# The opening of an attention stage re-dealt: four routed rows requested at once, late tiles, fills, loads and one batch's normalization put in other slots

## The reference, cut to what matters

```
x = x + tanh(g_xattn[0]) * quantized_linears(layernorm(x))
x = x + tanh(g_ffn[0])   * moe0(layernorm(x))       # 8 experts, top 2, and a shared expert for every row
x = x + tanh(g_xattn[1]) * attention(layernorm(x))  # q = x @ Wq, rope, 32 heads of 16, 512 keys, softmax, @ Wout + bout
x = x + tanh(g_ffn[1])   * moe1(layernorm(x))       # 8 experts, top 2
```

## Time and profile before

| | us |
|---|---|
| median of 3 runs | 1315.97 (1313.9 to 1318.4) |
| the profiled execution | 1319.94 |
| its span from first to last instruction | 1318.2 |
| attention block starts at | 561.8 |
| first reduction of the maxima | 623.06 |
| first scores, turn (0, 0) | 669.2 |

### The profile page before, as it was taken

How to read it: one execution, slowest core, us unless ns; L and a number is a source line. 1 busy time by engine, 2 the same in 40 slices (tenths; PEclk the granted TensorE clock), 3 DMA queues, 4 the chain that set the end, 5 groups by cost and what they waited for, 6 DMA issues and landing times.

```text
span 1318.2 us, 16527 instructions
## 1 busy us (share of the span) xinstructions
PE 1159.4 (88%) x5247; PEld 509.5 (39%) x5309; DVE 831.5 (63%) x1289; ACT 666.5 (51%) x1175; POOL 397.7 (30%) x469
## 2 busy tenths in 40 slices
PE   5777776899999999958799989999999999889997
PEld 3454443555444444423232223222322222224543
DVE  6798765235555554136978888777877777714543
ACT  2565554565222222236456666666656666763452
POOL 4466531002322222043234432222222223102332
PEclk8988898999999999988899999999999999999999
DMA  7424125644544444194324342222222225400101
GB/s 239 134 99 136 56 89 183 234 178 163 208 135 142 155 149 132 62 292 101 107 80 138 114 122 79 83 81 80 75 86 79 80 81 65 51 5 9 38 35 48
DMA packets 111029, 145.79 MB, mean 111 GB/s; under 512 B 24952, under 2 KB 79736, under 8 KB 110440
## 3 DMA queue, kind: packets, MB, share of 16 engines
q1 hardware_dynamic: 91816, 113.47, 26.7%
q0 software_dynamic: 18368, 28.85, 8.5%
q10 hardware_dynamic: 768, 2.49, 0.6%
HBM read 99.54 MB, written 48.37 MB: 112 GB/s over the span
## 4 chain that ended last, share of the span: by engine, by line
PE 32%; DVE 9%; issue 8%; ACT 7%; POOL 1%; DMA 1%; ACTq 0%; POOLq 0%; DVEq 0%
PE PS L2888 7%; PE PS L2854 5%; PE PS L2789 4%; PE PS L2873 4%; PE PS L2813 3%; DVE a_top L3223 3%; ACT shared_w L3010 2%; PE PS L2391 2%; PE PS L2414 1%; ACT a_E L3010 1%; DMA a_attnT<-f_y,l_pos 1%; POOL a_K L2151 1%; PE PS L2018 1%; DVE a_early L3096 1%; PE PS L1984 1%
## 5 line engine op out<-in xcount | busy, mean ns | idle before, releaser
L3223 DVE TENSOR_REDUCE a_top<-PS 128x2 f32<-128x1024 f32 x256 | 309.2, 1223 | 84.9 <-PE PS L2873 78.5
L3010 ACT ACTIVATE shared_w<-PS 128x512 f32<-128x512 f32 x256 | 138.9, 596 | 74.7 <-PE PS L2854 73.8
L2854 PE MATMUL PS<-a_Q,a_K 99*128 99x512 bf16 (+1 forms) x468 | 156.9, 387 | 15.7 <-ACT a_E L3010 3.4
L3010 ACT ACTIVATE a_E<-PS 128x512 f32<-128x512 f32 x256 | 138.8, 596 | 61.1 <-PE PS L2854 57.9
L1502 PE MATMUL PS<-f_W,f_GT 128*128 x312 | 141.3, 596 | 0.0
L2873 PE MATMUL PS<-a_K,a_Q 64*128 64x512 bf16 x512 | 100.8, 390 | 13.4 <-DVE a_top L3223 7.0
L1931 POOL TENSOR_TENSOR a_qf<-a_qf,a_tab 128x512 f32<-128x512 f32 x15 | 19.1, 1272 | 279.9 <-DVE a_swapped L3125 279.9
L2854 PEld LDWEIGHTS PS<-a_Q,a_K 99*128 99x128 bf16 (+1 forms) x512 | 44.1, 97 | 151.2 <-issue 49.6
L1558 DVE TENSOR_TENSOR f_H<-f_SG,PS 128x256 f32<-128x256 f32 x39 | 16.4, 421 | 115.3 <-ACT f_SG L1542 115.3
L1502 PEld LDWEIGHTS PS<-f_W,f_GT 128*128 128x128 f32 x312 | 56.7, 191 | 57.2 <-issue 57.2
L2789 PE MATMUL PS<-a_xT,a_early 128*128 128x512 f32 x128 | 72.4, 662 | 2.2 <-ACT a_qf L2982 0.8
(11 more groups left out here) (381 smaller groups left out, 2085.7 us busy)
## 6 DMA issues: line engine op xcount, KB each, us to landing
f0r_raw<-in_L_ffn_W_dram SPq DMA_DIRECT2D x24, 512.0 KB, 4.0
a_K<-k_parts SPq DMA_DIRECT2D x192, 64.0 KB, 2.3
a_Q<-a_q_parts SPq DMA_DIRECT2D x186, 64.0 KB
f_y<-f_Y SPq DMA_DIRECT2D x39, 256.0 KB, 2.0
v_units<-V SPq DMA_DIRECT2D x16, 512.0 KB, 2.9
a_V<-v_units SPq DMA_DIRECT2D x16, 512.0 KB, 3.5
k_parts<-f_k_parts SPq DMA_DIRECT2D x16, 384.0 KB, 3.4
a_q_parts<-a_parts SPq DMA_DIRECT2D x16, 384.0 KB, 2.8
```

Source lines behind the costliest of these rows:

```text
L2854: nc.tensor.matmul(PS[:, 4 + h % 2, :], K6[k][0:rows_, o, head // 2, kt * P:(kt + 1) * P], Q6[k][0:rows_, o, head // 2, :], start=True, st ...
L3010: nc.scalar.activation(E[step % 2][:, h, :], PS[:, 4 + h % 2, :], ACT.Exp).then_inc(exp_done, 1)
L3223: nc.vector.tensor_reduce(top[:, h - h % 2:h - h % 2 + 2, t], PS[:, 2 * pair:2 * pair + 2, :], AX.X, ALU.max).then_inc(maxed, 1)
```

## The change

The ring of routed rows gets a fourth slot, so that the gathers of tiles 0 to 3 are all requested at once; tiles 8 to 15 are added one turn later each. Batch 0 is measured and normalized before the loop, each `bn_stats` behind its tile. The late tiles' loads come in four pieces with a semaphore each. SyncE waits for tile 0 before it requests Wq, and for tile 2 before the bias (now first), the table, K, V and the late tiles' second load. The transposes of batch 0 alternate between banks 7 and 3. Late tile 2 stops after two of its ups before the loop; the tables `LATE` and `FILLS` are dealt anew, and ScalarE's six loads of q come at slot 4 behind the silus, instead of slot 3. Batch 1 is measured at slots 8 to 13 of turn (-1, 3), normalized at slots 4 to 7 of turn (0, 0), transposed at slots 8, 10, 12 and 14 there, its bias added in four pieces at slots 12 to 15.

```diff
 class LateTiles
-    DOWN = (6, 0, 1, 2, 6, 6, 6, 6)
+    DOWN = (6, 0, 1, 6, 6, 6, 6, 6)
     def load(self, sp, k):
-        sp.dma_start(self.homes[k], self.xT_dram[k]).then_inc(self.loaded[k], 16)
+        for c in range(self.DC):
+            sp.dma_start(self.homes[k][:, c, :], self.xT_dram[k][:, c, :]).then_inc(self.loaded[k][c], 16)
     def up(self, pe, n, c):
+        if t == 0:
+            pe.wait_ge(self.loaded[k][c], 16)
 attention
-        rows = Combine(..., 3, [attnT[1][:, d, :] for d in range(DC)])
+        rows = Combine(..., 4, [attnT[1][:, d, :] for d in range(DC)])
 jobs
-                for d, when in enumerate((6, 7, 8, 10)):
+                for d, when in enumerate((8, 10, 12, 14) if b == 0 else (6, 7, 8, 10)):
                     add(when, "x", (b + 1, 0), d)
-        LATE = {(-1, 0): {9: [("g", 2, 0), ("y", 0, 0), ("y", 1, 0), ("t", 2, 0)]},
-                (-1, 2): {4: downs(2) + ups(3), 5: [("g", 3, 0), ("y", 2, 0)] + ups(4), 6: [("t", 3, 0), ("g", 4, 0)] + downs(3),
-                          7: [("y", 3, 0), ("t", 4, 0)], 8: downs(4, [0]), 9: downs(4, [1]), 10: [("y", 4, 0)] + ups(5, [0]), 11: ups(5, [1]),
-                          12: ups(5, [2]), 13: ups(5, [3]), 14: [("g", 5, 0)], 15: [("t", 5, 0)]},
-                (-1, 3): {4: downs(5), 5: [("y", 5, 0)] + ups(6, [0]), 6: ups(6, [1]), 7: ups(6, [2]), 8: ups(6, [3]), 9: [("g", 6, 0)],
-                          10: [("t", 6, 0)] + ups(7, [0]), 11: ups(7, [1]), 12: ups(7, [2]) + downs(6, [0]), 13: ups(7, [3]),
-                          14: downs(6, [1]) + [("g", 7, 0)], 15: [("y", 6, 0), ("t", 7, 0)]},
+        LATE = {(-1, 0): {9: [("y", 0, 0), ("y", 1, 0)]},
+                (-1, 2): {4: ups(2, [2, 3]) + ups(3), 5: [("g", 2, 0), ("t", 2, 0)] + downs(2), 7: [("y", 2, 0), ("g", 3, 0)],
+                          8: [("t", 3, 0)] + ups(4, [0]), 9: downs(3), 10: ups(4, [1]), 11: [("y", 3, 0)] + ups(4, [2]),
+                          12: ups(4, [3]), 13: [("g", 4, 0)] + ups(5, [0]), 14: [("t", 4, 0)] + ups(5, [1]), 15: ups(5, [2])},
+                (-1, 3): {4: ups(5, [3]) + downs(4, [0]), 5: downs(4, [1]) + ups(6, [0]), 6: [("g", 5, 0), ("y", 4, 0)] + ups(6, [1]),
+                          7: [("t", 5, 0)] + ups(6, [2]), 8: ups(6, [3]) + downs(5, [0]), 9: downs(5, [1]),
+                          10: [("g", 6, 0), ("y", 5, 0)] + ups(7, [0]), 11: [("t", 6, 0)] + ups(7, [1]), 12: ups(7, [2]) + downs(6, [0]),
+                          13: ups(7, [3]) + downs(6, [1]), 14: [("g", 7, 0), ("y", 6, 0)], 15: [("t", 7, 0)]},
                 (0, 0): {0: downs(7), 1: [("y", 7, 0)]}}
 bank_of
+            if kind == "x" and unit[0] == 0:
+                return PS[:, (7, 3)[extra % 2], :]
 batch_to_norm
-            nb = {0: b + 1 if b == -1 else None, DC - 1: b + 2}.get(c)
+            nb = {0: b + 1 if b < 1 else None, DC - 1: b + 2 if b >= 0 else None}.get(c)
 sync
             late.load(sp, 0)
+            sp.wait_ge(rows.tile_added, 1)
             sp.dma_start(wq, ...)
+                    else:
+                        sp.wait_ge(rows.tile_added, TB - 1)
+                        sp.dma_start(tbias[:], bout.partition_broadcast(P)).then_inc(tbias_loaded, 16)
                     sp.dma_start(tab[0][:], ...)
                     load_kv(unit)
+                    late.load(sp, 1)
                     load_kv((0, 1))
-                if is_first(unit):
-                    sp.dma_start(tbias[:], bout.partition_broadcast(P)).then_inc(tbias_loaded, 16)
-                    late.load(sp, 1)
 tensor
+                    if b == 0 and extra >= 2:
+                        pe.wait_ge(xT_ready, extra - 1)
-                        pe.wait_ge(late.added, 3 + pair)
+                        pe.wait_ge(late.added, 3)
-            for c in range(DC):
+            for c in range(2):
                 late.up(pe, 2, c)
 scalar
-            FILLS = {(-1, 0): {11: [(1, 0)], 12: [(1, 1)], 13: [(1, 2)]}, (-1, 1): {4: [(1, 3)]},
-                     (-1, 2): {3: [(2, 0), (2, 1)], 8: [(2, 2)], 9: [(2, 3)], 10: [(3, 0)], 11: [(3, 1)], 12: [(3, 2)], 14: [(3, 3)]}}
+            FILLS = {(-1, 0): {11: [(1, 0)], 12: [(1, 1)]}, (-1, 1): {4: [(1, 2), (1, 3)]},
+                     (-1, 2): {9: [(2, 0)], 10: [(2, 1)], 11: [(2, 2)], 12: [(2, 3)]}, (-1, 3): {1: [(3, 0)], 3: [(3, 1)], 5: [(3, 2)], 8: [(3, 3)]}}
-            late.silu(act, 2)
-                    if (b, c, n) == (-1, 2, 3):
+                    if (b, c, n) == (-1, 2, 4):
                         act.wait_ge(q_stored, 16)
                         load_q(act, (0, 0), range(SLOTS // 2, SLOTS))
 vector
-            rows.vector(v, 0)
-            late.gate(v, 0)
-            rows.vector(v, 1)
-            late.gate(v, 1)
-            rows.vector(v, 2)
-            rows.vector(v, 3)
+            first_tile(0)      # rows.vector, wait for tile_added, bn_stats
+            first_tile(1)
+            late.gate(v, 0)
+            first_tile(2)
+            late.gate(v, 1)
+            first_tile(3)
+            ...                # bn_aggr x4, wait for the root, reciprocal, normalize x4
-                    pieces = whole if nb < 2 else [[t] for t in range(TB)]
+                    pieces = [[t] for t in range(TB)] if nb else [list(range(TB))]
```

More of the change, by code:

```diff
@@ L3021, in turn @@
                 for step in range(8):
[L3022 to L3025 removed]
+                    nb = batch_to_measure(b, c)
+                    if step == 3 and nb not in (None, 1):
+                        root(nb)
                     if (b, c, step) == (NB - 1, 2, 6):
@@ L3031, in turn @@
                     slot(2 * step)
+                    if step == 7 and nb == 1:
+                        root(1)
                     exps((b, c), step, (2, 3))
```

81 lines of the change are left out of this document (52 added, 29 removed).

## The result

The changed kernel takes 1308.01 us, median of 6 runs (1306.34 to 1315.7), beside 1316.33 for the kernel before (6 runs, 1313.9 to 1318.4). The ratio is 0.9948, interval 0.9929 to 0.9966: 8.3 us gained, where 17.4 was forecast. The time is inside the range, near its upper end; its value lies 1.2 us above that of rival B.

The account below looks back on a forecast made before the run. Bound: the string of waits from tile 3's late gather to the first reduction, which starts all later attention. 17.0 + 2.7 - 1.3 - 1.0 = 17.4 us gained, 1298.6 us for the median; range 1294 to 1309.

Parts of the forecast that it names:

- rival B: Late work comes back in full, 2.3 lost in part 4, 5.5 in part 5: 9.2 gained, 1306.8 us; chance 0.17.
- Part 1: Block's start until batch 0 is normalized: gathers issued back to back, ready at 582.0 instead of 593.0, 11.0 us gained.
- near bound: Landing of tile 3's second gather as in the block before: 4.1 us from issue, so at 575.5.
- far one: Landing of tile 3's second gather as slow as before: 9.9 us, so 581.3; then 6.5 gained instead of 11.0.
- Rival A: Opening: gathers no faster, batch 0 4.5 us later than forecast; gain 12, 1304 us; chance 0.20.
- Part 2: Transposes, q, swap: two banks and full clock, sum 5.8 us; swap at 589.6 instead of 606.57, 17.0 gained.
- Part 3: Parts ready to first reduction: 10.8 us instead of 11.2, 0.4 charged for SyncE's issues; first reduction at 606.1.
- rival C: TensorE idles before 602, then stays at 1.2 GHz through part 4, mean clock 0.64: 1332.6 us; chance 0.05.
- Part 4: First reduction to scores: TensorE and VectorE both at 39, times 1.116 is 43.5 us, 2.7 gained.
- Part 5: Given back: 1.3 us in turn (0, 0) for batch 1's normalizing, 1.0 in (1, 0) for two routed tiles.
- The rule on GpSimd's descriptors: Tiles 6 and 7's gathers beside the normalizing: issue stretches by up to 1.92 us; the sum stays.
- Rival D: Something other than tile 3 holds the first reduction at 623: within 4 us of before, 1314 us; chance 0.05.

Follow-up runs that it names:

- e12: The changed kernel once more, unaltered, profiled a second time; 1311.36 us, ratio 0.9957 to the kernel before.
- e5: The changed kernel with three slots for the routed rows instead of four, all else as changed; ratio 0.9962 to the kernel before.
- e4: The changed kernel with SyncE's order of before: no waits for tiles, bias behind K and V of two units; ratio 0.9996 to the kernel before.
- e10: The changed kernel without SyncE's waits for tiles, but with the bias ahead of table, K and V; ratio 0.9948 to the kernel before.
- e1: The changed kernel with K and V of unit (0, 1) requested behind SyncE's loads of q; 1309.7 us, ratio 0.9940 to the kernel before.
- e7: The changed kernel with tiles 8 to 15 added in turns (0, 0) to (0, 3) as before; 1309.86 us, ratio 0.9952 to the kernel before.
- e6: The changed kernel with batch 1 normalized in turn (-1, 3) and its root and copies placed as before; 1310.53 us, ratio 0.9953 to the kernel before.
- e13: The changed kernel with the edits of e1, e6 and e7 together; 1306.76 us, ratio 0.9918 to the kernel before.
- e9: The changed kernel with e1's and e6's edits, ScalarE's q loads behind late tile 2's copy, K and V of (0, 1) held until q landed; ratio 0.9934.

## Why the prediction was half right

**The reading of the bound** was right: the string from tile 3 to the first reduction set the start of everything behind it, and what was left of its gain at the end of turn (1, 0) arrived whole at the end of attention, 8.0 and 8.0.

**Part 1, batch 0 ready: 11.0 forecast, 9.3 measured.** Right in mechanism. The gather was issued where it was expected (8.76 us after the first, against 7 x 1.25 = 8.75), but took 7.05 to land, between the near bound of 4.1 and the far one of 9.9. I had taken 4.6. (In e12 the gain is 8.4.) Rival A, gathers no faster, is out: normalizing would have ended 4.5 later than forecast, and ended 1.7 later. What I credited to the slot is mostly the held loads': without the slot e5's 17.05 lies inside the scatter, without the holding tile 3 comes 3.1 (e4) and 1.8 (e10) later.

**Part 2, swap: 7.6 us of string forecast, 7.8 measured.** Right in each term: clock 1.00 from 585 to 592, a group 0.67 (0.66 taken), q 3.67 (3.70 taken), and VectorE's additions and bias just hidden, as long as the bias has landed. That condition was not in the prediction. e4 shows its price, 8.66.

**Part 3, parts to first reduction: 11.2 forecast (10.8 and the charge of 0.4), 14.9 measured.** This is the step that failed, 3.7 of the 9.4 missing. I did the sum for SyncE by its *issues*: they end at 596.1, 1.2 behind the parts, charge 0.4. The issues were no trouble: they ended at 593.84, 4.2 ahead of the parts at 598.07. What was late was the data. Thirteen loads stood in the queue ahead of the store, which took 6.2 us instead of the 2.5 that it takes without them (e1). ScalarE's six loads wait for that store with the late tile's copy queued behind them, TensorE idles 5.17, and the downs cost 3.78 instead of 1.98. The idle and the low clock were in rival C as a place, and C's condition (0.64 through the stretch) was far from met: 0.96.

**Part 4, to the scores: 2.7 gained forecast, 1.6 measured.** TensorE's busy time came out at 39.22 for 39.0, VectorE's at 37.19 for 38.5. The factor of 1.116 over the busiest engine became 44.56 / 39.22 = 1.136. At a clock of 1.00 the stretch takes 42.8 (e4, e5, e7) for the 43.5 forecast; at the 0.96 of this profile it missed by 1.1. VectorE's relief is worth 1.3 of it (e6).

**Part 5, given back: 2.3 forecast, 5.0 measured** (2.9 in turn (0, 0), 2.1 from the end of (0, 0) to that of (1, 0)). In (0, 0) the mechanism was named, normalizing ahead of the cut of the maxima. The 1.3 taken for it is about what is left when the clock is alike, though it was taken as the middle of a range; the rest of the 2.9 goes with a clock of 0.93, which the prediction didn't have. In (1, 0) the 1.0 for the two tiles' additions was wrong: they cost nothing (34.34 us in both kernels). Its going into the right direction was luck, since what turn (1, 0) gave back was low clock: from the end of (0, 0) to the end of (1, 0) e5, at a clock of 1.00 throughout, is 0.5 us longer than before, the changed kernel 2.1.

Rival B's upper ends for this part, 5.5, are near the 5.0, but not for its reason in (1, 0). It has part 4 wrong by 3.9 us (2.3 lost against 1.6 gained), and parts 1 to 3, which it took over, are short by 5.7. That the two nearly cancel makes its total come near the time.

**The rule on GpSimd's descriptors** changed nothing. Two gathers lay wholly or in part beside batch 0's normalizing, 582.92 to 584.95, and were issued in 0.95 and 1.03 us, against 0.94 and 0.95 for those at the block's start: at most 0.09 where the rule of the Trainium skill ("SBUF — State Buffer", SBUF: two separate sides) could have cost 1.92. The trace does not bear it out at this place.

**Rival D** is out: the first reduction moved by 11.3.

The sum: 9.3 + 5.8 (a string of 7.8 instead of 13.6) - 3.7 + 1.6 - 2.9 - 2.1 = 8.0.

Still open: what starts and ends the short spells of low clock that gave back part of every further gain, and why e13's six times agree within 1.1 us where those of the changed kernel spread over 7.5 to 9.4.

## What to carry to other kernels

When loads are moved later, do the sum for the bytes in front of the next dependent transfer on the same queue, not for the end of the issues: an issue that is on time can land several microseconds late. When one piece of a late string is sped up, list every operand of the following steps that was early enough only because the string was late (here the output's bias, 8.66 us). When you weigh an edit by one stretch, compare profiles whose granted clock is alike there: by the changed kernel's own 44.56 us VectorE's relief looks void, against runs at a clock of 1.00 it gains 1.3. And look at which instructions lie between two marks before you charge an interval to an edit: the additions suspected of 2.6 us stood behind the mark, and cost nothing.

## What the hardware showed beyond that

- A 384 KB store behind thirteen queued loads took 6.2 us to land (5.0 to 7.1 in six executions, each time 1.0 behind the last of the loads), 2.5 without these loads ahead of it. The last 64 KB load of q, in ScalarE's queue, took 5.74 us with SyncE issuing K and V right behind its own half of q (e1), 2.95 with K and V held back (e9).
- The same wait of 2.10 us of TensorE, at the same place in the same code, was followed by the lower clock level in the changed kernel (a pair of products 0.61 us, 0.90 over the interval) and not in e5 (0.39, and 1.00). Behind a wait of 5.17 us the downs took 3.78 instead of 1.98.
- The same program's last stage took 174.59 us at a granted clock of 1.00 and 179.10 at 0.97, with nothing in the kernel differing.
